# Adding the causal mask of the row maximum on the vector engine, packing the value products into 65 output columns a tile, and filling the query products from 96 to 128 rows

## What is computed

```python
q = rms_norm(x @ w_qa, q_a_norm_w) @ w_qb          # rank 96, then 16 heads of 192
kv_up = rms_norm(c_kv, kv_a_norm_w) @ w_kvb        # rank 64, then keys and values
scores = einsum('bhsd,bhtd->bhst', q_full, k_full) * scale
scores = where(tril, scores, finfo.min)
attn = softmax(scores, axis=-1)
out = einsum('bhst,bhtd->bhsd', attn, v)
```

## Time and profile before

| | |
|---|---|
| median of three runs | 1313.97 us (1307.87 to 1314.54) |
| the profiled execution: its time | 1310.41 us |
| its span | 1308.6 us |
| PE, PEld busy | 1182.8 us, 948.0 us |
| DVE, ACT, POOL busy | 880.5, 789.5, 692.6 us |
| granted TensorE clock, mean | 0.961 |

### The profile page before, as it was taken

One profiled execution on the slowest core, in us unless ns is written; L12 is line 12 of the kernel. 1 busy time (PEld: TensorE's weight loads), 2 busy tenths in 40 slices (PEclk: granted clock), 3 DMA queues, 4 the chain that ended last, 5 costly groups with the idle time before them and its releaser, 6 DMA issues. The chain is left out here.

```text
span 1308.6 us, 23936 instructions
## 1 busy us (share of the span) xinstructions
PE 1182.8 (90%) x9452; PEld 948.0 (72%) x9452; DVE 880.5 (67%) x1836; ACT 789.5 (60%) x1166; POOL 692.6 (53%) x569
## 2 busy tenths in 40 slices
PE   2856899999999999999999999999999867989897
PEld 2644577777777777777767777777878766878786
DVE  2533776677686777767677776767766567677776
ACT  1163467777777777777777777777787733222232
POOL 0121366767767666776766777666676742111100
PEclk9875699999999999999999999999999987999999
DMA  9202010000100200010020010002000050000000
GB/s 275 81 1 57 17 42 12 7 17 18 42 17 2 58 2 17 27 32 17 2 58 1 17 38 22 18 1 58 2 17 2 1 161 1 1 17 1 17 17 17
DMA packets 57679, 39.65 MB, mean 30 GB/s; under 512 B 7744, under 2 KB 57152, under 8 KB 57408
## 3 DMA queue, kind: packets, MB, share of 16 engines
q1 hardware_dynamic: 51216, 33.94, 8.8%
q10 hardware_dynamic: 6352, 4.19, 1.4%
HBM read 33.66 MB, written 4.46 MB: 29 GB/s over the span
## 5 line engine op out<-in xcount | busy, mean ns | idle before, releaser
L793 DVE TENSOR_REDUCE gates<-bank 128x1 f32<-128x512 f32 (+3 forms) x640 | 380.5, 608 | 210.4 <-PE bank L866 135.4
L685 POOL TENSOR_TENSOR pt_lo<-pt 128x1024 f16<-128x1024 f32 x192 | 375.2, 1964 | 213.4 <-ACT pt L742 213.3
L742 ACT ACTIVATE pt<-pair 128x1024 f32<-128x1024 f32 x192 | 196.2, 1022 | 131.0 <-PE pair L895 130.6
L733 ACT ACTIVATE pair<-shift 128x1024 f32<-128x1024 f32 x256 | 263.7, 1030 | 12.2 <-ACT pt L746 0.4
L909 PE MATMUL bank<-values,pt_lo 128*128 128x65 f16 x2176 | 225.4, 193 | 8.2 <-DVE rowsum L825 7.4
L911 PE MATMUL bank<-values,pt 128*128 128x129 f16 x2176 | 232.2, 220 | 0.0
L909 PEld LDWEIGHTS bank<-values,pt_lo 128*128 128x128 f16 x2176 | 185.4, 98 | 48.9 <-issue 27.9
L691 POOL TENSOR_TENSOR pt_lo<-pt 128x512 f16<-128x512 f32 (+3 forms) x256 | 179.1, 722 | 64.9 <-ACT pt L746 63.7
L911 PEld LDWEIGHTS bank<-values,pt 128*128 128x128 bf16 x2176 | 193.3, 98 | 0.0
L746 ACT ACTIVATE pt<-pair 128x512 f32<-128x512 f32 (+3 forms) x256 | 110.6, 436 | 63.8 <-PE pair L895 52.8
L895 PE MATMUL pair<-q_hi,kt_a_hi 128*128 128x512 f32 (+1 forms) x320 | 135.4, 423 | 0.0
(11 more groups left out here) (217 smaller groups left out, 2306.0 us busy)
## 6 DMA issues: line engine op xcount, KB each, us to landing
turn_by<-rope_cos_by_feature SPq DMA_DIRECT2D x64, 128.0 KB, 3.0
turn_by<-rope_sin_by_feature SPq DMA_DIRECT2D x64, 128.0 KB, 3.0
xs<-in_L_attn_x ACTq DMA_DIRECT2D x1, 2048.0 KB, 25.4
lat<-in_L_attn_w_o SPq DMA_DIRECT2D x1, 2048.0 KB, 26.6
xs_again<-in_L_attn_x SPq DMA_DIRECT2D x1, 2048.0 KB, 8.1
out<-xs_again SPq DMA_DIRECT2D x4, 512.0 KB, 2.8
lat<-in_L_wmod SPq DMA_DIRECT2D x1, 1536.0 KB, 15.9
lat<-in_L_attn_w_qb SPq DMA_DIRECT2D x1, 1152.0 KB, 8.1
```

The source lines that it names most:

```text
L685: pool.tensor_tensor(out=pt_lo[:, at].rearrange("p a n -> p (a n)"), in0=full, in1=cut(full), op=ALU.subtract).then_inc(low_ok, 1)
L733: act.activation(s_pair[u % 2][:, :, :], shift[:, item % SHIFTS:item % SHIFTS + 1, :].to_broadcast([P, 2, BW]), ACT.Copy).then_inc(seeded[ ...
L742: act.activation(pt[:, at], s_pair[u % 2][:, :, :], ACT.Exp).then_inc(exp_done, 1)
L793: dve.tensor_reduce(out=mx[:, item % MAXIMA, t, part:part + 1], in_=work_of(w)[:, 0:n * P], axis=AXX, op=ALU.max).then_inc(work_seen["v"], 1)
```

## The change

The diagonal chunk loses its mask matmul. DVE adds the mask while it takes the maximum: one instruction adds `mask16`, now 512 columns wide with the old tile at its end, to the chunk in PSUM, writes it back and reduces it with max. The chunks return to their plain order, since the function and the loop that placed the diagonal ones are gone.

In `weigh` the two matmuls of a tile become three: the high part of `pt` times the high values and the one (65 columns), the same weights once more times the low values (64 columns), and `pt_lo` times the high values and the one (65 columns). All add into the same 65 columns. The four tiles of an item stand in one PSUM bank, and the items take the two banks in turn. DVE empties an item's bank with one copy of 4 x 65 columns into `lat`, whose heads are now 65 columns wide; `rowsum` is gone, and `experts` reads the row sums from `lat`. PE's first value product of an item waits for the emptying of the item before the last.

`ql_hi`, `ql_lo` and the two `wq` tiles get 128 rows; four DVE memsets set rows 96 to 127 to zero, and the query products contract over 128 rows.

```diff
-def before_values(c):
-    r = CHUNK_ROUND[c]
-    return c == CHUNKS_AT[r][-1] and len(CHUNKS_AT[r]) > 1 and r not in SHIFT_AT and PREP_AT.get(r, (0, 3))[1] == 3
-for _k in range(NI):
...
-        CHUNKS[_c] = (_diagonal if _c in _places else _rest).pop(0)
-        lat = sb(stack, "lat", [P, NT, H * KVL])
-        rowsum = sb(stack, "rowsum", [P, NT, H])
+        lat = sb(stack, "lat", [P, NT, H * (KVL + 1)])
-        ql_hi = sb(attn, "ql_hi", [QL, S], F32R)
-        ql_lo = sb(attn, "ql_lo", [QL, S], F32R)
-        mask16 = sb(attn, "mask16", [P, P], BF16)
+        ql_hi = sb(attn, "ql_hi", [P, S], F32R)
+        ql_lo = sb(attn, "ql_lo", [P, S], F32R)
+        mask16 = sb(attn, "mask16", [P, BW], BF16)
+                for rest in (k["ql_hi"], k["ql_lo"]):
+                    dve.memset(rest[QL:, :].bitcast(F32), 0.0).then_inc(consts, 1)
-        wq = [sb(own, f"wq_pair_{p}", [QL, 3 * P], F32R) for p in ("hi", "lo")]
+        wq = [sb(own, f"wq_pair_{p}", [P, 3 * P], F32R) for p in ("hi", "lo")]
# DVE, maximum
-                    dve.tensor_reduce(out=mx[:, item % MAXIMA, t, part:part + 1], in_=work_of(w)[:, 0:n * P], axis=AXX,
-                                      op=ALU.max).then_inc(work_seen["v"], 1)
+                    of, to = work_of(w)[:, 0:n * P], mx[:, item % MAXIMA, t, part:part + 1]
+                    if part == ITEMS[item][1]:
+                        dve.tensor_tensor_reduce(out=of, in0=of, in1=mask16[:, BW - n * P:], scale=1.0, scalar=LOWEST, op0=ALU.add,
+                                                 op1=ALU.max, accum_out=to).then_inc(work_seen["v"], 1)
+                    else:
+                        dve.tensor_reduce(out=to, in_=of, axis=AXX, op=ALU.max).then_inc(work_seen["v"], 1)
# DVE, evacuate
-                    dve.tensor_reduce(out=lat[:, tiles, head * KVL:head * KVL + KVL],
-                                      in_=of[:, :, 0:2 * KVL].rearrange("p t (a n) -> p t n a", a=2), axis=AXX,
-                                      op=ALU.add).then_inc(o_seen, 1)
-                    dve.tensor_copy(rowsum[:, tiles, head:head + 1], of[:, :, 2 * KVL:2 * KVL + 1]).then_inc(o_seen, 1)
+                    dve.tensor_copy(lat[:, BT * g:BT * g + BT, head * (KVL + 1):head * (KVL + 1) + KVL + 1],
+                                    o_bank[item % 2][:, 0:BT * (KVL + 1)].rearrange("p (t n) -> p t n", t=BT)).then_inc(o_seen, 1)
+                for w in wq:
+                    dve.memset(w[QL:, :].bitcast(F32), 0.0).then_inc(consts_ok, 1)
-                    if r >= 2 and UNITS[r - 2][2] is not None:
+                    if r >= 2 and UNITS[r - 2][2] == 2:
                         evacuate(r - 2)
# PE, maximum
-                    last = pe.matmul(to[:, 0:cols], q, kt_hi[h][:, part * BW:part * BW + cols], start=True, stop=not diagonal)
-                    if diagonal:
-                        last = pe.matmul(to[:, (n - 1) * P:n * P], ident16[:, :], mask16[:, :], start=False, stop=True)
-                    last.then_inc(work_done, 1)
+                    pe.matmul(work_of(w)[:, 0:cols], q, kt_hi[h][:, part * BW:part * BW + cols], start=True,
+                              stop=True).then_inc(work_done, 1)
# PE, weigh
-                    if u == FIRST_UNIT[item] and item > 0:
-                        pe.wait_ge(o_seen, 4 * item)
+                    if u == FIRST_UNIT[item] and item > 1:
+                        pe.wait_ge(o_seen, item - 1)
-                            pe.matmul(to[:, col + KVL:col + 2 * KVL + 1], pt_lo[:, at, half, mine], values[:, j + half, KVL:2 * KVL + 1],
-                                      start=(u == FIRST_UNIT[item] and half == 0 and t % 2 == 0), stop=False, skip_group_check=True)
-                            last = pe.matmul(to[:, col:col + 2 * KVL + 1], cut(pt[:, at, half, mine]),
-                                             values[:, j + half, 0:2 * KVL + 1], start=False, stop=end, skip_group_check=True)
+                            low_values, with_one = values[:, j + half, 0:KVL], values[:, j + half, KVL:2 * KVL + 1]
+                            pe.matmul(to, cut(pt[:, at, half, mine]), with_one, start=(u == FIRST_UNIT[item] and half == 0 and t == 0),
+                                      stop=False, skip_group_check=True)
+                            pe.matmul(to[:, 0:KVL], cut(pt[:, at, half, mine]), low_values, start=False, stop=False,
+                                      skip_group_check=True)
+                            last = pe.matmul(to, pt_lo[:, at, half, mine], with_one, start=False, stop=end, skip_group_check=True)
# experts
-                    dve.reciprocal(rden[:, tiles, :], rowsum[:, tiles, :]).then_inc(rden_ok, 1)
+                    dve.reciprocal(rden[:, tiles, :], lat[:, tiles, :].rearrange("p t (h n) -> p t h n", h=H)[:, :, :, KVL]).then_inc(rden_ok, 1)
```

More of the change, by code:

```diff
@@ L42 @@
 BW = BT * P
+MASK_AT = BW - P
 SCALE = 1.0 / math.sqrt(DN + DR)
@@ L45 @@
 MASKED = -1.0e30
+LOWEST = -3.0e38
 P_SCALE = 1024.0
@@ L141 @@
 SEEDS = {e: [0, *itertools.accumulate(seed_on_vector(u) == (e == "v") for u in range(NU))] for e in "av"}
-ENDS = [0, *itertools.accumulate(d is not None for _, _, d in UNITS)]
 def adaln_block_kernel(nc, x, w_qa, q_norm, w_qb, w_kva, kv_norm, w_kvb, w_o, w_gate, wi_0, wi_1, wo, c, wmod,
@@ L271, in block_of @@
         def block_of(w, n, b):
-            return w[:, bass.ds(b * BW, BW)]
+            return w[0:QL if n == 2 else P, bass.ds(b * BW, BW)]
         def product_of(n):
@@ L311, in _ @@
                 pool.memset(values[:, :, 2 * KVL:], 1.0).then_inc(consts, 1)
-                pool.wait_ge(consts, 5)
+                pool.wait_ge(consts, 7)
                 for m in (ident, ident16):
@@ L315, in _ @@
                                        pattern=[[-1, P]], channel_multiplier=1).then_inc(consts, 1)
-                pool.affine_select(out=mask16[:, :], in_=mask16[:, :], compare_op=ALU.is_ge, fill=MASKED, base=0,
+                pool.affine_select(out=mask16[:, MASK_AT:], in_=mask16[:, MASK_AT:], compare_op=ALU.is_ge, fill=MASKED, base=0,
                                    pattern=[[-1, P]], channel_multiplier=1).then_inc(consts, 1)
@@ L506, in _ @@
             def _(pe):
-                pe.wait_ge(consts, 8)
+                pe.wait_ge(consts, 10)
                 pe.wait_ge(wscaled, 1)
@@ L592, in attend @@
 def attend(nc, sb, sem, k):
-    bank, lat, rowsum, ident, wq_dram, values = k["bank"], k["lat"], k["rowsum"], k["ident"], k["wq_dram"], k["values"]
+    bank, lat, ident, wq_dram, values = k["bank"], k["lat"], k["ident"], k["wq_dram"], k["values"]
     ident16, mask16 = k["ident16"], k["mask16"]
@@ L657, in _ @@
                         for part in range(2):
-                            sp.dma_start(wq[part][:, :].bitcast(F32), wq_dram[part, hp]).then_inc(wq_in, 16)
+                            sp.dma_start(wq[part][0:QL, :].bitcast(F32), wq_dram[part, hp]).then_inc(wq_in, 16)
                     if p > 1:
@@ L885, in scores @@
                             on = (d + n) * P
-                            pe.matmul(s_pair[u % 2][:, n, on:on + P], mask16[:, :], ident16[:, :], start=False, stop=False,
+                            pe.matmul(s_pair[u % 2][:, n, on:on + P], mask16[:, MASK_AT:], ident16[:, :], start=False, stop=False,
                                       skip_group_check=True)
@@ L940, in experts @@
 def experts(nc, sb, sem, k):
-    bank, lat, rowsum, ident, gates = k["bank"], k["lat"], k["rowsum"], k["ident"], k["gates"]
+    bank, lat, ident, gates = k["bank"], k["lat"], k["ident"], k["gates"]
     modc, neg_half, turnstile = k["modc"], k["neg_half"], k["turnstile"]
@@ L1059, in normalise_sums @@
                     tile = bass.ds(f * BT + t, 1)
-                    pool.tensor_tensor(out=lat_n[:, t % 2], in0=lat[:, tile, :].rearrange("p a (h n) -> p (a h) n", h=H),
+                    pool.tensor_tensor(out=lat_n[:, t % 2], in0=lat[:, tile, :].rearrange("p a (h n) -> p (a h) n", h=H)[:, :, 0:KVL],
                                        in1=rden[:, tile, :].rearrange("p a h -> p (a h)").unsqueeze(2).to_broadcast([P, H, KVL]),
```

7 lines of the change are left out of this document (2 added, 5 removed).

## The result

The changed kernel takes 1302.56 us (median of 4 runs, 1301.42 to 1304.19) against 1313.1 us for the kernel before in the same comparison: ratio 0.993, 95% interval 0.9906 to 0.9955. It is 10.5 us faster, where 18 to 19 were forecast (1295 us); the range of 1280 to 1311 us holds it.

A forecast was written before the change was run, and what follows sets the result against it. The prediction took PE's stream to bound the stage from 200 to 1040 us. Its terms, -21 + 2 + 11 - 8 - 3 - 1 + 2, came to -18 us, forecasting 1295 us, range 1280 to 1311.

The forecast's parts named there:

- last sign: Attention stage: the forecast is wrong if the stage from 200 us on does not end about 18 us earlier.
- Part 1: Scores on PE: removing 256 mask matmuls gives -21 us, bounds -17 and -25; dropping the chunk placing costs nothing.
- Part 2: Masked maximum on DVE: 0.1 us more per read, mostly hidden, felt before shifts and query products; +2 us, bounds 0 and +7.
- Part 3: Value products in `weigh`: three short matmuls a tile and less of the fp32 load hidden behind them; +11 us together.
- Part 4: Emptying and bank per item: -8 us from PE's wait for the emptying, -3 us from waits before shifts.
- Parts 5 and 6: Query products over 128 rows instead of 96: -1 us; edges of the launch (memsets, queue, `experts` reading `lat`): zero.
- Part 7: Feeding PE: its sequencer hands on 1920 more matmuls and short rounds may run dry; +2 us, bounds 0 and +10.
- A: Value products: short matmuls cannot follow each other that fast; at 43 ns each, +94 us, some 1384 us; chance 0.12.
- B: Masked maximum: the new DVE instruction is dear, 0.5 us over the reduce, giving 1307 to 1320 us; chance 0.08.
- C: Query products: row count matters, wider ones gain 0.1 to 0.3 us at 96 places, 1275 to 1285 us; chance 0.05.
- D: Attention stage: time saved turns into PE's waits before shifts, query products and values, leaving 1300 to 1309 us; chance 0.1.

The follow-up runs named there:

- mask_only: The kernel before with the mask added in DVE's maximum and no mask matmul, chunks in the old placing: 1298.45 us, ratio 0.9903.
- weigh_only: The kernel before with three value matmuls a tile, a bank per item and the single emptying copy, mask still on PE: 1309.48 us, ratio 0.9986.
- widen_only: The kernel before with the query products over 128 rows and nothing else: 1312.86 us, ratio 0.9998.
- after_wait_each_item: The changed kernel with an item's first value product waiting for the emptying of the item just before: 1316.59 us, ratio 1.0031.
- after_plain_reduce: The changed kernel with the diagonal chunks' maximum taken by the plain reduce, without the mask: 1299.25 us, ratio 0.9892.

## Why the prediction was right, and where it was not

It said faster, and was 7.6 us too low at the median. That it came so near is partly luck. Of the 10.5 us between the medians only 6.2 are the stage's, a third of the 18; 2.2 are the earlier start and the shorter tail of the profiled pair, and 2.1 are what the medians differ beyond that pair, none of which the prediction had a term for. By its own last sign (the stage ends about 18 us earlier) it was wrong: the last value product starts 7.7 us earlier. Measured in the stage:

- **Part 1, the mask matmul (-21 us)**: `mask_only` shows -12.8 together with the new DVE work. If that costs there the 8 us that it costs in the plain order, the matmuls gave -21; the two were not measured apart in the old order, where PE's wait for `rowsum` grew by 4.5 us as well. The sentence behind the term is the step that failed: "The planner's placing of chunks becomes worthless with the matmul, so its removal costs nothing beside." It costs **8.0 and 8.7 us** in two pairs of kernels. I read from the lines what the placing was for, and not what stood where afterwards: it had also kept the narrow chunks away from the place directly ahead of shifts and query products, where they leave DVE no time for the full chunk before them. With it back, the gap ahead of shifts is 3.2 us shorter, ahead of chunks 1.4 and ahead of query products 1.3. The first and the last are what this explains, 4.5 of the 8.0 us; the rest is spread over many steps, and its cause is open.
- **Part 2, the DVE maximum (+2 us)**: mis-sized. The instruction is cheaper than I took (0.06 us over the reduce, 0.1 in the sum), but the stage pays **8 us**. I counted only the diagonal reads before shifts and query products; most of the 8 us stands before and behind other chunks and at the seed mask, where DVE's lateness shows as well.
- **Part 3, three short matmuls (+11 us)**: +14.4 by PE's steps (90 ns a tile by the medians of the three steps, with the first after fp32 work at 40 ns; 88.5 were taken), +10 to +11 net. The second fp32 product comes 0.346 us behind the last short matmul, as said.
- **Part 4, the bank per item (-8, -3 us)**: 9.4 us come back with the wait, in stalls of about 1.18 us. In `weigh_only` the gap ahead of shifts shrinks by 2.5 us and ahead of chunks by 1.8. Both as forecast.
- **Parts 5 and 6**: the rows give nothing. The 0.236 us that the term took for a product of 96 rows is the median with 128 rows too. Of the edges the stage's start shows nothing: it comes at 116.0 us against 117.5, and its first product waits for its weights' DMA as before.
- **Sum.** -13.1 us for the three parts with the old placing, +8.0 for the lost placing: -5.1, against -6.2 measured. The forecast's -18 misses the 8 of the order and, if Part 1's matmuls gave their -21, 6 of the DVE maximum; the 2 of Part 7 are inside what Part 3 measured.

**Rivals.** A is refuted: 28 to 33 ns a step. The Trainium skill (TensorE: Matmul & The Clock Gate, Back-to-back issue gap) gives 81 ns for each load and matmul at 128 columns; it is not seen here either, where the step over a 129-column matmul is 57 ns in the kernel before. Two sums of the rivals were off: the gain of 18 us is gone from 8 ns a tile on, 32 ns a matmul, and not from 11 and 33; and 0.1 to 0.3 us at 96 places would have given C 1266 to 1285 us. B's mechanism was there in small: the instruction isn't dear, but DVE's time is less well hidden than its 246 idle us suggest. C is refuted by `widen_only`. D's number came true (1300 to 1309), and its mechanism in part: the waits before shifts and query products grew by 2.2 us and those of chunks for DVE by 5.5, but the wait for the emptying is gone.

## What to carry to other kernels

Before a helper that orders work is deleted because its purpose is gone, list what stands ahead of every wait with it and without it: an order can be good by accident, and here it was worth 8 of the 14 us that the change gives with it. Where consumers take turns in two buffers, a step waits for the read of the work two ahead, so put the shortest read there and a long work behind it: moving four chunks an item took 20 us off the plain order and 12 off the old one, with no instruction added or removed. And an engine that is idle 30% of the time can still charge the bottleneck: 0.06 us more on each of 256 reads, 15 us in all, cost the stage 8.

## What was not expected of the hardware

**The tail has two lengths.** From the last value product to the end the thirteen profiled executions take either 257.6 to 258.9 us (six, before and after among them) or 262.4 to 263.7 us (seven), whatever was changed in the stage before. One place of the tail, some 110 us behind the last value product, in the changed kernel and in `after_wait_each_item` (columns as in the earlier trace rows; each row of ten us):

```profile
1152.50:1162.50 10.00, 6.89 (x48) 6.08 (x47) 8.78 (x23) 2.32 (x4) 1.91 (x1) 1.00 0.00 0
1162.50:1172.50 10.00, 10.00 (x76) 9.52 (x76) 5.99 (x15) 2.32 (x4) 0.00 (x0) 1.00 0.01 2
```

```profile
1162.10:1172.10 10.00, 6.87 (x44) 6.08 (x43) 8.29 (x22) 2.30 (x4) 1.91 (x1) 0.89 0.00 0
1172.10:1182.10 10.00, 10.00 (x58) 9.52 (x58) 4.49 (x10) 1.45 (x4) 0.00 (x0) 0.76 0.01 2
```

PE is busy alike, 6.9 of 10 us and then all of them, but its granted clock stays at 1.00 in one and falls to 0.89 and 0.76 in the other, that is to 1.2 GHz for a part of the 20 us, and it gets 58 matmuls done where the first has 76. Ahead of the fall PE had been idle for 3 of 10 us in both. Over the whole tail the clock stands at 1.2 GHz for 28.1 us in the first and for 45.6 in the second, for 28 to 37 us in the six short tails and 45 to 50 in the seven long ones. The difference of 5 us is as much as several of the edits: the spans of `after_plain_reduce` and `after_wait_each_item` look 5 us worse than their stages. That the medians carry it too is likely, as they show the same 3 to 5 us, but only the profiled executions show their tails. What decides between the two was not found.

**A 16-bit matmul of 64 or 65 columns with its own load of 128x128 steps in 28 to 33 ns** (medians of the three steps of a tile), for 24 in a row.
